# Last six layers: gate and value products of the feed-forward as three fp32r products each, with shared buffers and new orders

## The chip, the cores and the metric

One NeuronCore of a Trainium2 chip runs the whole program. The metric is the device time of one execution in microseconds; lower is better. The engines are TensorE (PE), VectorE (DVE), ScalarE (ACT), GpSimd (POOL) and the sync engine (SP), which only issues DMA transfers here. Each engine works through its own list of instructions in order and is held up by semaphores alone.

## The reference, cut to what matters

The model has four stages on a stream of 4 batches x 512 tokens x 128 features. The change touches the last one, a stack of six layers of windowed attention and gated feed-forward:

```
def ffn_layer(x, g, bln, W1, b1, W2, b2):           # W1: 128 x 682, W2: 341 x 128
    xn = (x - mean) / sqrt(var + 1e-05) * g + bln
    a, gate = split(xn @ W1 + b1, 2)                # two halves of 341 columns
    return a * gelu(gate) @ W2 + b2
for i in range(6):                                   # DEPTH
    x = attn_layer(shift_tokens(x), Wqkv[i], ...) + x    # 16 heads of 64, windows of 32 keys
    x = ffn_layer(shift_tokens(x), ...) + x
```

`shift_tokens` takes half of the features from the token before. All tensors are float32.

## The kernel before

`windowed_layers` (line 1509) holds the six layers. A **round** is one layer for one batch of 512 tokens, so there are 24 rounds; features lie on the partitions. Each engine has a hand-written cyclic order, the table `ORDER`; a word in it is a unit of work, and the dashes behind it say how many rounds late it is: in iteration i of the table, `g0--` works on round i-2. So up to four rounds are under way at once, and the function `turns` walks the table. The units of a round are:

- `P t.j`, `V t.j` (PE, line 1785): queries and keys, and values, of token tile t, four and two products of 128 tokens x 512 columns into the two PSUM banks `psP`. Each is computed as three fp32r products, x_hi·w_hi + x_lo·w_hi + x_hi·w_lo. fp32r is a float32 rounded so that one pass suffices. `w_hi`/`w_lo` and `xh`/`xl` are these splits: a rounded copy by ACT (1858, 1863), and the difference by POOL (2037, 2042).
- `Sq`, `R`, `AB`, `ad`, `Ra`, `nm`: norms and rotary embedding of queries and keys, on ACT, DVE and POOL; `Ve` (ACT) copies the values out. `T t.j` (PE, 1794) transposes the result and `Te` (ACT) copies it out.
- `S k` (PE, 1803 and 1812): scores of 64 queries; `Xm`, `Xe`, `Xd`, `Xn`: maximum (DVE), exponentials (ACT, 1893), sum (DVE), division (POOL, 2071). `At k` (PE, 1823) transposes the probabilities, `Pt` (ACT) copies them out, `Av k` (PE, 1841) multiplies by the values, `Ot` (ACT, 1906) copies out. The transposes of `T` and `At` share one bank `psT`; `Av` has one bank pair `psO`, which `Ot` must have emptied before the next `Av`.
- The tail of a round goes through a single bank `psF`, one after the other: `wo0`, `wo1` (PE, 1729, output projection), `xf` (DVE, residual sum), `xfd` (SP, loads the shifted tokens), `tr` (PE, 1736), `ls`, `lr`, `ln` (layer norm on DVE and POOL), `back` (PE, 1740), `xn` (ACT, 1911), then for each of three column blocks k of 128, 128 and 85 columns `g`k (PE, 1751, gate), `gg`k (ACT, 1917, Gelu, preceded by a load of its table), `a`k (PE, 1751, value), `h`k (DVE, 1994), and at the end `w2` (PE, 1755) and `out` (DVE, 1998).
- SP: `VE k` copies values shifted by 32 tokens into the two buffers `v_even` (lines 1702, 1704; `X` is their name in the profile), `xd` loads the next input of `xh`, `tl` loads `w_o` (1582), `t1` loads the feed-forward weights (1586 to 1588), `wd` loads the next layer's qkv weights.
- The gate and value products at line 1751 are plain float32: one instruction in the code, two records in the profile.

## Time and profile before

| | us |
|---|---|
| three runs | 2397.17, 2399.85 (median), 2401.15 |
| the profiled execution, whole | 2398.7 |
| its span, first to last instruction | 2396.9 |
| PE busy in the span | 2203.9 (92%) |
| ACT busy | 1719.1 (72%) |
| DVE busy | 1780.6 (74%) |
| POOL busy | 1230.9 (51%) |

Busy shares are means over four very different stages. The last stage fills the page's 40 slices from about the 13th on; there the page's PE row shows 9 in nearly every slice and the clock row 9. The ends of matmuls are modelled, so that neighbours overlap in the records; how much room a unit takes on PE is the distance from its start to the next one's.

### The profile page before, as it was taken

To read this page: it belongs to the slowest core of one execution; us is meant where nothing else is said; L and a number is where in the kernel's file an instruction comes from. 1 tells how busy PE (TensorE), PEld (TensorE's weight loads), DVE (VectorE), ACT (ScalarE), POOL (GpSimd) and SP (SyncE) were. 2 spreads that over 40 slices of the span, in tenths; PEclk is the share of its full clock that TensorE was granted. 3 is DMA by queue.
4 is the path that set the end of the run, shared out by engine and by line. 5 is a ranking of instruction groups with operands and counts; after the bars stand their busy time and mean duration, and the time that the engine had idled before them with its cause. 6 is when DMAs were issued, how large, how long until landed. Compare 5 with 4: busy or idle time off the path is not lost.

```text
span 2396.9 us, 82108 instructions
## 1 busy us (share of the span) xinstructions
PE 2203.9 (92%) x33332; PEld 1567.5 (65%) x33332; DVE 1780.6 (74%) x3567; ACT 1719.1 (72%) x3982; POOL 1230.9 (51%) x2002
## 2 busy tenths in 40 slices
PE   6799679999976799999999999999999999999996
PEld 3487368888855566666766666666666666666662
DVE  3577377777777788888888888878888888888851
ACT  2255378888854678878888787777778888778771
POOL 0177010000001677776777776767777777767650
PEclk9899789999987899999999999999999999999997
DMA  2000021221102111112111121112111211122110
GB/s 88 10 1 1 22 98 53 80 80 53 71 2 82 30 51 51 51 47 58 51 53 42 54 72 48 45 44 60 50 41 39 75 53 51 36 64 60 40 33 22
DMA packets 40966, 117.73 MB, mean 49 GB/s; under 512 B 7952, under 2 KB 13392, under 8 KB 37776
## 3 DMA queue, kind: packets, MB, share of 16 engines
q1 hardware_dynamic: 40592, 112.49, 15.5%
q8 instruction: 265, 4.34, 0.8%
q14 instruction: 109, 0.89, 0.1%
HBM read 50.48 MB, written 2.23 MB: 22 GB/s over the span
## 4 chain that ended last, share of the span: by engine, by line
PE 49%; ACT 10%; issue 4%; POOL 2%; DVE 2%; DMA 1%; SPq 0%; ACTq 0%; POOLq 0%; DVEq 0%
PE w_psP L1785 12%; PE w_psT L1794 7%; PE w_psF L1729 6%; PE w_psO L1841 6%; PE w_psS L1812 5%; PE w_psF L1751 5%; PE w_psT L1823 3%; ACT w_pb L1893 3%; PE w_psF L1755 2%; PE w_psS L1803 2%; ACT w_sq L1868 1%; ACT L1893 1%; ACT L1917 1%; DMA w_xsf<-H 1%; ACT w_oT L1906 1%
## 5 line engine op out<-in xcount | busy, mean ns | idle before, releaser
L2055 POOL TENSOR_TENSOR w_ab<-w_ab,w_nrm 128x512 f32<-128x512 f32 x384 | 392.9, 1045 | 8.4 <-POOL w_nrm L84 8.4
L1893 ACT ACTIVATE w_pb<-w_psS,w_mx 128x64 f32<-128x64 f32 x1536 | 350.2, 338 | 2.8 <-DVE w_mx L1962 1.9
L2047 POOL TENSOR_TENSOR w_ab<-w_ab,w_bb 128x512 f32<-128x512 f32 x192 | 245.3, 1278 | 172.8 <-DVE w_bb L1946 171.1
L1958 DVE TENSOR_REDUCE w_nrm<-w_sq 128x8 f32<-128x512 f32 x384 | 249.5, 665 | 107.5 <-ACT w_sq L1868 107.3
L1868 ACT ACTIVATE w_sq<-w_psP 128x512 f32<-128x512 f32 x384 | 237.4, 618 | 84.7 <-DVE w_nrm L1958 42.5
L1785 PE MATMUL w_psP<-w_hi,w_xh 128*128 128x512 f32 x576 | 274.6, 477 | 25.0 <-POOL w_xl L2037 8.5
L2071 POOL TENSOR_TENSOR w_pb<-w_pb,w_sm 128x512 f32<-128x512 f32 x192 | 200.3, 1043 | 185.0 <-DVE w_sm L1971 184.5
L1794 PE MATMUL w_psT<-tables_all,w_ab 128*128 128x128 f32 x1536 | 242.0, 280 | 8.7 <-POOL w_ab L2055 4.0
L1197 DVE TENSOR_TENSOR e_glo<-e_hh,e_ghi 128x512 fp32r<-128x512 f32 x256 | 169.3, 685 | 93.0 <-ACT e_ghi L1151 92.9
L1794 PEld LDWEIGHTS w_psT<-tables_all,w_ab 128*128 128x128 f32 x1536 | 174.2, 141 | 87.3 <-ACT w_qT L1881 23.9
L1785 PE MATMUL w_psP<-w_lo,w_xh 128*128 128x512 f32 x576 | 231.1, 401 | 0.0
L1785 PE MATMUL w_psP<-w_hi,w_xl 128*128 128x512 f32 x576 | 229.3, 398 | 0.0
L1145 ACT ACTIVATE e_hh<-e_psH,e_cols 128x512 f32<-128x512 f32 x256 | 175.4, 686 | 55.4 <-PE e_psH L1067 54.0
L1341 POOL MEMSET a_sc<- 128x256 f32 (+2 forms) x6 | 2.9, 524 | 385.0 <-POOLq L314 385.0
L1899 ACT ACTIVATE w_pT<-w_psT 128x512 f32<-128x512 f32 x192 | 120.5, 628 | 77.0 <-PE w_psT L1823 74.1
L1950 DVE TENSOR_TENSOR w_bb<-w_psP,w_tabs 128x512 f32<-128x512 f32 x192 | 131.6, 685 | 58.6 <-ACT w_sq L1868 49.1
L1812 PE MATMUL w_psS<-w_kT,w_qT 64*32 64x64 f32 x12288 | 168.7, 225 | 5.1 <-issue 4.9
L1729 PE MATMUL w_psF<-w_oT,w_o 128*128 128x512 f32 x384 | 172.5, 592 | 0.9 <-DVE H L1998 0.9
L1751 PE MATMUL w_psF<-w_hh,w 128*128 128x512 f32 (+1 forms) x288 | 155.4, 622 | 7.1 <-ACT w_yn L1917 3.5
L1881 ACT ACTIVATE w_qT<-w_psT 128x512 f32<-128x512 f32 x192 | 115.6, 602 | 64.3 <-PE w_psT L1794 64.2
L1885 ACT ACTIVATE w_kT<-w_psT 128x512 f32<-128x512 f32 x192 | 116.5, 607 | 55.5 <-PE w_psT L1794 55.5
L1812 PEld LDWEIGHTS w_psS<-w_kT,w_qT 64*32 64x32 f32 x12288 | 135.5, 106 | 30.3 <-issue 7.3
(294 smaller groups left out, 5348.5 us busy)
## 6 DMA issues: line engine op xcount, KB each, us to landing
X<-tables_layer SPq DMA_DIRECT2D x48, 384.0 KB, 3.5
X<-w_v SPq DMA_DIRECT2D x48, 384.0 KB, 3.5
e_gb<-gate_rows SPq DMA_DIRECT2D x16, 1024.0 KB, 4.7
e_raw<-in_w_moe SPq DMA_DIRECT2D x32, 256.0 KB, 5.1
w_raw<-in_w_qkv SPq DMA_DIRECT2D x20, 384.0 KB, 4.8
X<-tables_layer SPq DMA_DIRECT2D x48, 128.0 KB, 3.6
w_o<-in_w_o SPq DMA_DIRECT2D x6, 512.0 KB, 4.6
w_xs<-H SPq DMA_DIRECT2D x24, 128.0 KB, 3.3
```

What stands on the lines that cost most here:

```text
L1145: act.activation(hh[b % 2][:, j, :], psH[j][:, :], ACT.Gelu, bias=b1(e, j)).then_inc(s["hh"], 1)
L1729: last = pe.matmul(psF[:, :], w_o[:, pair, :], oT[:, pair, :], start=(pair == 0), stop=(pair == PAIRS - 1), skip_group_check=True)
L1751: last = pe.matmul(psF[0:m, :], w_1[:, at:at + m], xn[:, :], start=True, stop=True)
L1785: last = pe.matmul(psP[u % 2][:, :], x[r % 2][:, tt], w[:, layer % 2, ww], start=(n == 0), stop=(n == len(terms) - 1))
L1794: last = pe.transpose(psT[:, 128 * q:128 * (q + 1)], ab[:, k % 2, j, 128 * q:128 * (q + 1)], c.ident[:, :])
L1812: last = pe.matmul(psS[QB * c4:QB * c4 + QB, h, slot:slot + KEYS], qT[t % 2][rows, 4 * g + c4, at:at + QB], kT[rows, 4 * g + c4, 128 * t + ...
L1868: act.activation(sq[:, i % 2, :], psP[j % 2][:, :], ACT.Square).then_inc(s["sq"], 1)
L1893: last = act.activation(pb[k % 2][:, n, :], psS[:, j, KEYS * q:KEYS * (q + 1)], ACT.Exp, bias=mx[:, n:n + 1])
L1958: dve.tensor_reduce(nrm[k // 2][:, 0, 8 * (i % 8):8 * (i % 8) + 8], sq[:, i % 2, :].rearrange("p (h d) -> p h d", d=DH), AX_X, ALU.add).th ...
L2047: pool.tensor_tensor(a, a, bb[:, i % 2, :], ALU.add).then_inc(s["ad"], 1)
L2055: pool.tensor_tensor(a, a, nrm[k // 2][:, 1, 8 * (i % 8):8 * (i % 8) + 8].unsqueeze(2).to_broadcast([128, 8, DH]), ALU.mult).then_inc(s["n ...
L2071: pool.tensor_tensor(p, p, sm[k % 2][:, :].unsqueeze(2).to_broadcast([128, PAIRS, KEYS]), ALU.mult).then_inc(s["pn"], 1)
```

## The change

The gate and value products `g`k and `a`k become three fp32r products each, like `P` and `V`. For that the layer's `w_1` is split once per layer into `w1_hi` (unit `fh`, ACT) and `w1_lo` (unit `fl`, POOL), and the normalised input of each round into `xn_hi` (unit `xnh`, ACT, a second evaluation from PSUM) and `xn_lo` (unit `xnl`, POOL, the float32 `xn` less `xn_hi`). `g`k now waits for all four. To make room, raw `w_1` is loaded into the space of `hh`, `xn` and the third block of `hh` lie in the space of `yn`, the scratch of the layer norm ahead of the stage lies in `ab`, and two unused tables with their memsets go. All five order tables are new.

```
     xsf = c.sb("w_xsf", [D, N])
-    hh = c.sb("w_hh", [D, 3, N])
-    xn = hh[:, 2, :]
+    hh = c.sb("w_hh", [D, 2, N])
+    xn = gg
+    w_1 = hh[:, :, :].rearrange("p a b -> p (a b)")[:, 0:2 * FF]
+    h_at = (hh[:, 0, :], hh[:, 1, :], gg)
+    xn_hi = c.sb("w_xnh", [D, N], F32R)
+    xn_lo = c.sb("w_xnl", [D, N], F32R)
...
# PE, one line of its table, before and after
-            P1.1 Av2.0- S6.0- At4.0- P1.2 back-- Av3.0- At5.0- P1.3 g0-- S7.0- Av4.0- V1.0 a0-- At6.0-
+            T3.3- S5.0- At3.0- Av2.0- back-- P1.1 S6.0- At4.0- P1.2 Av3.0- At5.0- P1.3 g0-- S7.0- Av4.0-
# SP
-            VE2.0-- xd0.0 VE3.0-- wd0.0- t1-- VE0.0- tl- VE1.0- xfd--""",
+            VE3.0--- xfd--- tl-- xd0.0 VE0.0-- t1--- VE1.0-- VE2.0-- wd0.0-""",
...
                 if f[0] == "g":
-                    pe.wait_ge(s["wf"], (layer + 1) * 48)
-                    pe.wait_ge(s["xn"], r + 1)
+                    pe.wait_ge(s["fh"], layer + 1)
+                    pe.wait_ge(s["fl"], layer + 1)
+                    pe.wait_ge(s["xnh"], r + 1)
+                    pe.wait_ge(s["xnl"], r + 1)
                     wait(pe, s["hh"], 3 * r + k)
...
-                last = pe.matmul(psF[0:m, :], w_1[:, at:at + m], xn[:, :], start=True, stop=True)
+                for n, (w, x) in enumerate(((w1_hi, xn_hi), (w1_hi, xn_lo), (w1_lo, xn_hi))):
+                    last = pe.matmul(psF[0:m, :], w[:, at:at + m], x[:, :], start=(n == 0), stop=(n == 2))
...
+                elif kind == "fh":
+                    if b == 0:
+                        wait(act, s["out"], r)
+                        act.wait_ge(s["wf"], (layer + 1) * 48)
+                        act.activation(w1_hi[:, :], w_1, ACT.Copy).then_inc(s["fh"], 1)
+                elif k == "xnh":
+                    act.wait_ge(s["f"], r * 10 + 3)
+                    wait(act, s["out"], r)
+                    act.activation(xn_hi[:, :], psF[:, :], ACT.Identity, bias=cols[:, 1:2],
+                                   scale=cols[:, 0:1]).then_inc(s["xnh"], 1)
...
+                elif kind == "fl":
+                    if b == 0:
+                        pool.wait_ge(s["fh"], layer + 1)
+                        pool.tensor_tensor(w1_lo[:, :], w_1, w1_hi[:, :], ALU.subtract).then_inc(s["fl"], 1)
+                elif k == "xnl":
+                    pool.wait_ge(s["xn"], r + 1)
+                    pool.wait_ge(s["xnh"], r + 1)
+                    pool.tensor_tensor(xn_lo[:, :], xn[:, :], xn_hi[:, :], ALU.subtract).then_inc(s["xnl"], 1)
```

**PE, from the gate product g0 to the value product a0**, in a round of the second layer. Before (S7 is 1803 with 1812, Av4 and later Av5 are 1841, V is 1785, At6 is 1823):

```order
L1751 MATMUL w_psF<-w_hh,w 128x512
L1803 MATMUL w_psS<-band_bf,ident_bf 128x256 x2
L1812 MATMUL w_psS<-w_kT,w_qT 32x64 x32
L1841 MATMUL w_psO<-w_pT,X 64x32 x32
L1785 MATMUL w_psP<-w_hi,w_xh 128x512
L1785 MATMUL w_psP<-w_hi,w_xl 128x512
L1785 MATMUL w_psP<-w_lo,w_xh 128x512
L1751 MATMUL w_psF<-w_hh,w 128x512
```

After (lines are 10 higher; 1761 is the split product, 1833 is At6, 1851 is Av4 and Av5):

```order
L1761 MATMUL w_psF<-w_xnh,w_1h 128x512
L1761 MATMUL w_psF<-w_xnl,w_1h 128x512
L1761 MATMUL w_psF<-w_xnh,w_1l 128x512
L1813 MATMUL w_psS<-band_bf,ident_bf 128x256 x2
L1822 MATMUL w_psS<-w_kT,w_qT 32x64 x32
L1851 MATMUL w_psO<-w_pT,X 64x32 x32
L1833 MATMUL w_psT<-tables_all,w_pb 128x128 x4
L1795 MATMUL w_psP<-w_hi,w_xh 128x512
L1795 MATMUL w_psP<-w_hi,w_xl 128x512
L1795 MATMUL w_psP<-w_lo,w_xh 128x512
L1851 MATMUL w_psO<-w_pT,w_v 64x32 x32
L1761 MATMUL w_psF<-w_xnh,w_1h 128x512
```

At6 and Av5 have moved in between g0 and a0; the product itself is three instructions.

**ACT, from Ot2 (1906) to the first Gelu load (1917)**, before:

```order
L1906 ACTIVATE w_oT<-w_psO 128x2x8x32
L1858 ACTIVATE w_xh<-w_xs 128x512
L1899 ACTIVATE w_pT<-w_psT 128x512
L1893 ACTIVATE w_pb<-w_psS,w_mx 128x64 x4
L1868 ACTIVATE w_sq<-w_psP 128x512
L1911 ACTIVATE w_hh<-w_psF,w_cols 128x512
L1893 ACTIVATE w_pb<-w_psS,w_mx 128x64 x4
L1899 ACTIVATE w_pT<-w_psT 128x512
L1868 ACTIVATE w_sq<-w_psP 128x512
L1906 ACTIVATE w_oT<-w_psO 128x2x8x32
L1917 ACT_TABLE_LOAD
```

After, from Pt3 (1909) on (1931 is xn, 1926 is xnh, 1916 is Ot2 and Ot3, 1903 the exponentials):

```order
L1909 ACTIVATE w_pT<-w_psT 128x512
L1931 ACTIVATE w_yn<-w_psF,w_cols 128x512
L1878 ACTIVATE w_sq<-w_psP 128x512
L1926 ACTIVATE w_xnh<-w_psF,w_cols 128x512
L1916 ACTIVATE w_oT<-w_psO 128x2x8x32
L1909 ACTIVATE w_pT<-w_psT 128x512
L1903 ACTIVATE w_pb<-w_psS,w_mx 128x64 x8
L1878 ACTIVATE w_sq<-w_psP 128x512
L1916 ACTIVATE w_oT<-w_psO 128x2x8x32
L1878 ACTIVATE w_sq<-w_psP 128x512
L1909 ACTIVATE w_pT<-w_psT 128x512
L1937 ACT_TABLE_LOAD
```

xh has left this stretch (it stands behind the second Gelu now), xnh has come into it, and xn comes one score unit earlier.

**SP, around the load of the shifted tokens w_xsf**, before:

```order
L1708 DMA w_xsf<-H 64x512
L1709 DMA w_xsf<-H 64x511
L1702 DMA X<-w_v 96x1024
L1704 DMA X<-tables_layer 32x1024
L1685 DMA w_xs<-H 64x512
L1686 DMA w_xs<-H 64x511
```

After, in a round where a layer begins (X<-tables_layer 96x1024 is VE0, w_hh is the raw w_1):

```order
L1715 DMA w_xsf<-H 64x512
L1716 DMA w_xsf<-H 64x511
L1692 DMA w_xs<-H 64x512
L1693 DMA w_xs<-H 64x511
L1709 DMA X<-tables_layer 96x1024
L1593 DMA w_hh<-in_w_ff 128x682
L1594 DMA w<-in_w_ff 128x384
```

w_xs and VE0 now stand behind w_xsf, and VE0, which stood a good half round ahead of it, is read by Av0 in the same round.

## Rows read from the trace of the kernel before

**Rows 1.** Page, part 4: share of the chain that ended last, by engine.
```profile
PE 49%; ACT 10%; issue 4%; POOL 2%; DVE 2%; DMA 1%; SPq 0%; ACTq 0%; POOLq 0%; DVEq 0%
```

**Rows 2.** Windows: stretch, us, PE, PEld, DVE, ACT, POOL busy (count), clock, DMA, GB/s.
```profile
1408.66:1434.29 25.63, 24.47 (x595) 18.14 (x594) 20.72 (x40) 24.72 (x63) 18.45 (x37) 1.00 0.19 54
1434.29:1472.56 38.27, 38.18 (x660) 26.06 (x659) 32.36 (x60) 26.96 (x69) 28.45 (x35) 1.00 0.16 44
1399.94:1463.83 63.89, 62.65 (x1252) 44.18 (x1250) 53.07 (x98) 51.68 (x131) 46.90 (x71) 1.00 0.17 48
```

**Rows 3.** Chain in order of time, 1400 to 1480: start, us, what.
```profile
1404.70 0.44 PE w_psF L1736 x4
...
1436.98 0.86 PE w_psF L1751 x2
...
1444.63 1.39 PE w_psP L1785 x6
...
1468.59 0.44 PE w_psF L1736 x4
```

**Rows 4.** Timeline of PE: start, us, instructions, [idle time before <-what ended it].
```profile
1415.90 1.14 PE L1841 MATMUL w_psO<-w_pT,X 64*64 64x32 f32 x64
1417.21 0.28 PE L1803 MATMUL w_psS<-band_bf,ident_bf 32*128 32x256 bf16 x2 [0.18 <-ACT w_pb L1893]
...
1419.93 1.14 PE L1841 MATMUL w_psO<-w_pT,tables_layer 64*64 64x32 f32 x64
1421.00 0.66 PE L1823 MATMUL w_psT<-tables_all,w_pb 128*128 128x128 f32 x4
...
1426.27 0.30 PE L1841 MATMUL w_psO<-w_pT,X 64*64 64x32 f32 x2 [0.94 <-issue]
...
1461.52 0.60 PE L1794 MATMUL w_psT<-tables_all,w_ab 128*128 128x128 f32 x4
```

**Rows 5.** Groups by line: operation, shapes, count | busy us, mean ns | idle.
```profile
L1858 ACT ACTIVATE w_xh<-w_xs 128x512 fp32r<-128x512 f32 x24 | 17.6, 733 | 1.6 <-DMA w_xs<-H 1.6
L1863 ACT ACTIVATE w_hi<-w_raw 128x768 fp32r<-128x768 f32 x20 | 17.1, 855 | 0.0
L2037 POOL TENSOR_TENSOR w_xl<-w_xs,w_xh 128x512 fp32r<-128x512 f32 x24 | 30.6, 1274 | 3.7 <-ACT w_xh L1858 3.7
L2042 POOL TENSOR_TENSOR w_lo<-w_raw,w_hi 128x768 fp32r<-128x768 f32 x20 | 36.8, 1839 | 18.6 <-ACT w_hi L1863 18.5
L1994 DVE SCALAR_TENSOR_TENSOR w_hh<-w_psF,w_cols,w_yn 128x512 f32<-128x512 f32 (+1 forms) x72 | 53.5, 743 | 33.7 <-PE w_psF L1751 33.5
```

**Rows 6.** Timeline of ACT: the table load and the first Gelu of a round.
```profile
1423.84 1.28 ACT L1917 ACT_TABLE_LOAD   x1
1425.13 0.69 ACT L1917 ACTIVATE w_yn<-w_psF,w_cols 128x512 f32<-128x512 f32 x1
```

**Rows 7.** Timeline of POOL: the division Xn5, and the scaling that T2.0 needs.
```profile
1418.68 1.04 POOL L2071 TENSOR_TENSOR w_pb<-w_pb,w_sm 128x512 f32<-128x512 f32 x1
...
1460.06 3.05 POOL L2055 TENSOR_TENSOR w_ab<-w_ab,w_nrm 128x512 f32<-128x512 f32 x3 [0.17 <-POOL w_nrm L84]
```

**Rows 8.** Waits of PE, 900 to 2244: total us, times, longest.
```profile
PE w_psP L1785 <- ACT tables_layer L1875: 5.1, 13, 0.5
...
PE w_psF L1736 <- DMA w_xsf<-H: 3.4, 3, 1.5
```

**Rows 9.** DMA issues by line: count, KB each, median us from issue to landing.
```profile
X<-tables_layer SPq DMA_DIRECT2D x48, 384.0 KB, 3.5
...
w_o<-in_w_o SPq DMA_DIRECT2D x6, 512.0 KB, 4.6
```

**Rows 10.** Line 1702 alone: spread of the time from issue to landing.
```profile
DMA to landing us min/median/max: 3.4/3.5/5.6
```

**Rows 11.** Timeline of PE in the last round, at half the clock.
```profile
2371.07 2.04 PE L1751 MATMUL w_psF<-w_hh,w 128*128 128x512 f32 x2 [0.97 <-issue]
```

**Rows 12.** Timeline of SP: the two loads of the shifted tokens.
```profile
1462.44 0.50 SPq L1708 DMA_DIRECT2D w_xsf<-H  x1
1462.99 0.59 SPq L1709 DMA_DIRECT2D w_xsf<-H  x1
```

65 lines of the change are left out of this document (33 added, 32 removed).

## Prediction, made before the changed kernel ran

> **What bounds the kernel now.** I read the chain of work first, then the last stage by windows, then one round of it unit by unit. The chain belongs to PE for 49% of the whole span, ACT follows with 10% [rows 1]. In the last stage it is tighter. One round takes 63.9 us: the transposes `tr` of two rounds in a row stand in the chain at 1404.70 and 1468.59 [rows 3]. In such a round PE is busy for 62.65 of 63.89 us, DVE 53.07, ACT 51.68, POOL 46.90, at the full clock [rows 2]. So a microsecond taken from PE's work in a round is worth up to a microsecond. But the windows show two phases: from 1434 to 1472 PE is busy for 38.18 of 38.27 us and ACT for 27 of 38, so there PE alone sets the pace; from 1408.66 to 1434.29 ACT is busy for 24.72 of 25.63 us [rows 2]. The tight phase, 1408 to 1434, holds half of the exponentials, the Gelus 0 and 1 with their table loads, and four of the six gate and value products; there PE waits for ACT as soon as ACT gets more to do. A saving of PE outside it is paid out in full, one inside only as far as ACT allows.
>
> **The products.** A float32 product takes 0.86 us of PE in the chain, two P units behind each other 1.39 us, so one triple of fp32r products takes 0.69 us [rows 3]. The triple is the very form that the change uses, in the same shapes, 24 times a round, so its price is not in doubt. Saved: 6 x (0.86 - 0.69) = 1.0 us a round. Behind a transpose the P unit pays some 0.08 us more for its first weights; only a2 gets such a neighbour, so I leave that out. At half the clock, where the last round's six products run (2.04 us of record each [rows 11]), the saving doubles to about 0.34 us each, 2.0 us in all.
>
> Here a rule says more than the row. The Trainium skill, "FP8 and Floating Point Precision", section TensorE Precision Notes, has it that true FP32 takes four passes through the array (high and low halves, all four combinations), and three products of the reduced form then cost three quarters: 0.86 x 0.75 = 0.65 us, an estimate. By it the saving would be 6 x 0.21 = 1.3 us a round instead of 1.0; the row's 0.69 us for three passes decides, and the sum goes by it.
>
> **Neighbours on PE.** Av2 is followed by S6, and S6 starts 1.31 us after it; Av3 is followed by At5, which starts 1.07 us after it [rows 4]. The new order has no S behind an Av: 0.24 us less a round. The rest of PE's units are the same, with about as many transposes behind an S or an Av. Together PE's own work shrinks by 1.0 + 0.24 = 1.24 us a round.
>
> **New work on ACT and POOL.** `xnh` costs what `xh` does, 0.73 us, `xnl` 1.27 us like `xl`, `fh` somewhat less than 0.86 us and `fl` than 1.84 us (682 instead of 768 columns) [rows 5]. ACT goes to 51.7 + 0.7 + 0.8/4 = 52.6 us in a round, POOL to 46.9 + 1.3 + 0.4 = 48.6: both still under PE. What counts is the tight phase. There `xh` (0.73) moves out, to behind the second Gelu, and `xnh` (0.73) moves in, so ACT's load in it stays the same, but for `fh` in one round of four. `g0` waits for xn, xnh, xnl: after `back` that is about 0.8 + 0.7 + 1.3 = 2.8 us, and the order now puts P1.1, S6, At4, P1.2, Av3, At5 and P1.3 between them, over 5 us, where before it was Av3, At5 and P1.3. On POOL `xnl` stands behind Xn5, which ended at 1419.72 (1418.68 + 1.04 [rows 7]), 1.3 us ahead of At5 at 1421.00 [rows 4], and At5 and P1.3 come before g0: `xnl` is hidden. Queued behind it on POOL are ad1.0 and Xn6; POOL is busy for only 18.45 of the 25.63 us [rows 2]. Were g0 late, all of PE would stand behind it, S7 first. Cost of these: nothing. `fh` waits for the load of w_1, which SP issues right behind VE0, some 20 units ahead, and which lands some 3 us later; queued behind `fh` is the copy of V0.1, that frees a bank for P1.1. In the six rounds with `fh` and `fl` ACT has no room for them; half to all of fh's 0.8 us shows, taken 0.5 each: +3 us, between 0 and 5 (with fl's 1.6 us hidden ahead of Xn5, or half of it not).
>
> **New waits.** I walked one round with the units' durations from the timelines, and three places come out late. (a) T2.0 now follows wo1 directly, since V3.0 has moved behind it, so it comes 0.77 us sooner; the scaling on POOL that it needs runs from 1460.06 and is done after a third of its 3.05 us, at 1461.1, and T2.0 started at 1461.52 [rows 4, 7]: slack 0.4, wait 0.4 us. (b) g1 and a1 stood three units apart (Av5, T0.0, P2.1), now two (T0.0, Av6); Gelu 1 waits for its table, 1.28 + 0.69 us [rows 6], behind exponentials and Ot5. My walk gives a wait of 0.8 us before a1, and At7 and P2.1 are queued behind it. Against it, P2.0 no longer waits for the copy of V1.0 (13 times, 0.4 us each [rows 8]), since Av5 now stands between; and stalls like the 0.94 us in which PE had no instruction in Av4 [rows 4] are absorbed by the same slack. (c) g2 needs h1 (0.74 us [rows 5]) and comes 1.8 us after a1 instead of 3.6; T0.2 stands behind `xh` and `wh` on ACT: 0.3 us. Together 1.5 us of new waits, against about 1.1 us of waits in the same stretch before. Taken: +0.4 us a round, between -0.3 (the walk adds up delays that in fact overlap) and +1.2 (none of the old waits goes).
>
> **SP.** VE0, the copy that Av0 reads, stood half a round ahead and now stands behind w_xsf and w_xs. The two loads of w_xsf take 1.1 us to issue and begin when xf is done [rows 12]; w_xs takes as long and some more, and VE0 lands 3.5 us after its issue [rows 9]. By hand: xf is done 1.1 us after the end of wo1, the loads of w_xsf and w_xs are issued by 3.9, VE0 lands at 7.4, and PE arrives at Av0 at 7.8 (thirteen units): hidden by 0.4 us. In the five rounds with a load of w_o (4.6 us, 512 KB [rows 9]) w_xsf no longer stands behind it, which cost `tr` 3.4 us in three rounds [rows 8], but Av0 will wait instead: 0 in sum, between -3 and +8.
>
> **Edges.** First rounds: two memsets less, nothing. Last round: the six products give 2.0 us, `xnh` and `xnl` lie bare, 0.7 + 1.3 = 2.0 us: 0.
>
> **Sum.** Per round -1.0 - 0.24 + 0.4 = -0.84 us; over 23 rounds (the last one stands by itself above) -19.3; +3 for fh and fl. That is -16 us on the profiled execution's 2398.7 (span 2396.9 and 1.8 around it), 1.2 under the median of 2399.85. On the median: 2383.5; forecast **2383**.
>
> **Rivals.**
> 1. *The new waits don't come*: each new one falls into the shadow of another, and all of PE's 1.24 us and a little of the old waits is won, 1.5 us a round: 23 x 1.5 = 35 less 3 gives 2368. For it: PE stands idle for only 1.2 us in a round [rows 2], and most waits are single ones that feed each other. Against: ACT's 96% in the tight phase.
> 2. *ACT sets the pace*: what PE wins in the tight phase turns into waits for Gelu and exponentials, and `xnh` comes on top. Four of the six savings lost, 0.7 us, and 0.5 us more in waits: -1.24 + 0.7 + 0.5, with the fh rounds nothing: 2399. For it: 24.72 of 25.63. Against: load there is equal.
> 3. *VE0 comes late*, slower than before. If the three loads ahead of it slow its landing from 3.5 to the 5.6 us that the longest took [rows 10], Av0 waits 2.1 - 0.4 = 1.7 us in every round: -0.84 + 1.7 = +0.9, over 23 rounds +20, with fh +3: 2423. It decides from a landing of about 4.7 us on (0.84 + 0.4 over 3.5). Against: the four longest are single ones, the median is 3.5 with neighbours on the queue.
> 4. *The split product is no cheaper here*: excluded, the same instructions stand 576 times in the trace.
>
> **How the numbers follow.** Forecast's own range 2374 to 2393, chance 0.60; rival 1 0.22 (2362 to 2374); rival 2 0.10 (2393 to 2405); rival 3 0.08. The range that should hold 8 in 10 leaves out rival 3, most of 2 and the far half of 1: 2366 to 2395. A measurement here can tell 0.2%, 4.8 us, from no change: faster means under 2395.0. Chances: faster 0.83, same 0.09, slower 0.08.
>
> **What would show it.** Right: the triple at 0.69 to 0.77 us from start to start; a round of about 63.0 us between `tr` units; S6 behind At or P at no extra; short waits before a1 and T2.0. Rival 1: rounds near 62.4. Rival 2: ACT busy for over 97% of the stretch from Pt2 to the second Gelu, and more waits of PE for ACT. Rival 3: Av0 waits for the DMA of w_v or tables_layer in most rounds. Wrong altogether: a wait of g0 for POOL, or Gelu table loads beyond four a round.

## The result: 2.2% slower, and where the time went

The changed kernel takes 2451.97 us (median of 4 runs, 2450.23 to 2456.31), the kernel before 2398.51 (2395.68 to 2401.15): ratio 1.0221, 95% interval 1.0201 to 1.0242. Forecast were 2383 us. The profiled execution took 2456.31 us (span 2454.7).

The loss lies in the last six layers. From the first P0.0 of the stage to the P0.0 of round 23 it was 1477.4 us in the trace of before (766.9 to 2244.3) and is 1530.1 now (770.3 to 2300.4): 52.7 us more. This length, called the stage below, serves for all kernels; it is from one profiled execution each.

The page of the changed kernel, part 1 (busy us, share, instructions), part 3 (DMA queues: packets, MB, share) and part 4 (the chain, which answers to [rows 1]):

```profile
PE 2203.2 (90%) x33476; PEld 1611.9 (66%) x33476; DVE 1787.5 (73%) x3567; ACT 1747.1 (71%) x4012; POOL 1273.5 (52%) x2030
...
q8 instruction: 267, 4.37, 0.7%
...
PE 36%; ACT 18%; issue 7%; DVE 5%; DMA 2%; POOL 1%; SPq 1%; ACTq 0%; POOLq 0%; DVEq 0%
```

PE's share of the chain fell from 49% to 36%, and 7% of it is "issue": PE waits for nothing that the profile shows. The waits of PE from 900 to 2240 us (total, times, longest; answers to [rows 8]) say where:

```profile
PE w_psO L1851 <- issue: 38.9, 43, 2.9
PE w_psO L1851 <- DMA X<-tables_layer: 12.3, 5, 2.9
PE w_psF L1736 <- DVE H L2018: 10.4, 20, 0.5
PE w_psF L1761 <- ACT w_yn L1937: 9.3, 20, 0.6
```

The first of these was 8.7 us in 11 waits before:

```profile
PE w_psO L1841 <- issue: 8.7, 11, 1.9
```

Line 1851 is the product of the weights with the values (`Av`), 64 small products in a unit. The timeline of PE (start, us, instructions, idle time before) and three stretches of it by windows (columns as in [rows 2]):

```profile
1439.33 0.32 PE L1851 MATMUL w_psO<-w_pT,tables_layer 64*64 64x32 f32 x2 [2.28 <-issue]
...
1502.95 0.40 PE L1795 MATMUL w_psP<-w_lo,w_xh 128*128 128x512 f32 x1
1503.28 0.28 PE L1813 MATMUL w_psS<-band_bf,ident_bf 32*128 32x256 bf16 x2
1503.49 0.29 PE L1822 MATMUL w_psS<-w_kT,w_qT 64*32 64x64 f32 x3
1504.07 0.83 PE L1822 MATMUL w_psS<-w_kT,w_qT 64*32 64x64 f32 x61 [0.28 <-issue]
1504.83 0.66 PE L1833 MATMUL w_psT<-tables_all,w_pb 128*128 128x128 f32 x4
1505.41 1.13 PE L1851 MATMUL w_psO<-w_pT,tables_layer 64*64 64x32 f32 x62
1509.12 0.24 PE L1851 MATMUL w_psO<-w_pT,tables_layer 64*64 64x32 f32 x2 [2.58 <-issue]
...
1576.32 0.24 PE L1851 MATMUL w_psO<-w_pT,tables_layer 64*64 64x32 f32 x2 [1.75 <-issue]
```
```profile
1439.33:1509.12 69.79, 65.08 (x1256) 47.46 (x1256) 54.54 (x101) 53.26 (x132) 50.75 (x74) 0.96 0.17 46
...
1438.80:1445.60 6.80, 6.27 (x21) 5.08 (x21) 3.14 (x8) 2.98 (x8) 2.82 (x3) 0.50 0.03 10
1510.50:1513.90 3.40, 3.39 (x11) 2.72 (x11) 0.44 (x1) 2.53 (x8) 0.08 (x1) 0.50 0.00 0
```

PE does 62 of the 64 products of Av1, stands for 1.5 to 2.9 us with two left, and goes on. No semaphore stands inside a unit, so this is no wait for data. It happens in 17 of the 24 rounds, always at this product. After 14 of these 17 stops the granted clock is 0.5, the lower level, for some microseconds (here for 6.8 us from 1438.8 and for 3.4 us from 1510.5), and what PE does there takes up to twice as long. From 900 to 2240 us PE spends 51 us at that level, against 7 us before. In the first round of each layer the stop is missing; there Av0 waits 2.0 to 2.9 us for the copy VE0 instead. And wo0 waits half a microsecond in nearly every round for `out`, behind Xd0.0 on DVE.

The mechanism stands in the numbers of the page. The queue "instruction" moved 4.37 MB in 267 packets, 16.4 KB each. PE's queue holds 33476 products, as many weight loads and some 1450 instructions that only wait: 68,400 in all, so 64 bytes each and 256 to a packet. Between two stops there are 1256 products and 1256 weight loads (the window from 1439.33 to 1509.12 above) and 48 waiting instructions: **2560, ten times 256**. Before, a round had 1250 of each and 45: 2545. The six triples bring 12 instructions more, the new waits 3. So the ends of the packets, which moved on by 15 instructions each round before, now stand at the same places in every round, and one of them is the 62nd product of Av1. The 256 instructions up to there (most of S4, At2, and Av1 to its 62nd product) are only 2.5 us of work.

In all 17 stops of this kind PE went on 1.3 to 1.6 us after the last 16 KB packet had landed (at 1507.76 for 1509.12). That the 256 are so short is not enough for a stop: in the first rounds of the layers the same 256 took 2.2 to 3.0 us, and PE ran on. There the packet had started 0.2 to 2.0 us before PE came to the 256 (PE had just waited for VE0), in the 17 stops it started 1.4 to 2.9 us after. So "held up by semaphores alone", as the section on the chip has it, leaves out the supply of instructions.

The Trainium skill, "Runtime: NRT & Kernel Launch", section Instruction fetch mechanics, says that the sequencer fetches blocks of 16 KiB, 256 instructions; the trace agrees. It also says that the cost of crossing such a boundary is "mostly hidden"; here it is not, with 1.5 to 2.9 us at a time.

Not all of the 38.9 us is this. Counted over all units of PE, idle times that end just behind a packet's end (at instruction 192 to 195 of a 256, 1.2 to 1.6 us after a packet had landed) are 34.1 us from 900 to 2240 us, for 14.2 us before, where units other than Av were hit as well. Another 5.6 us stand at the first product of Av3, 0.2 to 0.4 us in nearly every round, where no packet ends: Av3 starts there 0.1 us after the copy Ot2 on ACT, which the new `xnh` pushes back. The profile calls both "issue".

### The profile page after: what moved, and what is told of

It reads as the page before. It is cut to its first block, busy times and chain, and to the rows that moved or that the text cites. A ratio compares the mean times of both kernels' runs of the same rounds, so it can differ in the third digit from the quotient of the medians.

```text
span 2454.7 us, 82554 instructions
## 1 busy us (share of the span) xinstructions
PE 2203.2 (90%) x33476; PEld 1611.9 (66%) x33476; DVE 1787.5 (73%) x3567; ACT 1747.1 (71%) x4012; POOL 1273.5 (52%) x2030
## 3 DMA queue, kind: packets, MB, share of 16 engines
q8 instruction: 267, 4.37, 0.7%
## 4 chain that ended last, share of the span: by engine, by line
PE 36%; ACT 18%; issue 7%; DVE 5%; DMA 2%; POOL 1%; SPq 1%; ACTq 0%; POOLq 0%; DVEq 0%
PE w_psP L1795 10%; PE w_psF L1736 7%; PE w_psT L1804 6%; ACT w_pb L1903 5%; PE w_psS L1822 4%; PE w_psO L1851 3%; PE w_psF L1761 3%; ACT w_sq L1878 3%; ACT L1903 2%; PE w_psT L1833 2%; ACT L1937 2%; ACT w_pT L1909 2%; ACT w_yn L1937 1%; DMA X<-tables_layer 1%; PE w_psS L1813 1%
## 5 line engine op out<-in xcount | busy, mean ns | idle before, releaser
L1978 DVE TENSOR_REDUCE w_nrm<-w_sq 128x8 f32<-128x512 f32 x384 | 256.1, 674 | 61.0 <-ACT w_sq L1878 61.0
L1878 ACT ACTIVATE w_sq<-w_psP 128x512 f32<-128x512 f32 x384 | 246.2, 641 | 53.3 <-PE w_psP L1795 25.4
L1804 PE MATMUL w_psT<-tables_all,w_ab 128*128 128x128 f32 x1536 | 250.0, 287 | 9.1 <-ACT w_qT L1891 4.0
L1804 PEld LDWEIGHTS w_psT<-tables_all,w_ab 128*128 128x128 f32 x1536 | 184.1, 145 | 86.6 <-ACT w_qT L1891 28.0
L1795 PE MATMUL w_psP<-w_lo,w_xh 128*128 128x512 f32 x576 | 236.3, 410 | 0.0
L1795 PE MATMUL w_psP<-w_hi,w_xl 128*128 128x512 f32 x576 | 234.9, 408 | 0.0
L1982 DVE TENSOR_REDUCE w_mx<-w_psS 128x8 f32<-128x512 f32 x192 | 130.5, 680 | 81.6 <-PE w_psS L1822 81.4
L1989 DVE TENSOR_REDUCE w_sm<-w_pb 128x8 f32<-128x512 f32 x192 | 130.7, 681 | 43.8 <-ACT w_pb L1903 41.7
L1155 ACT ACTIVATE e_ghi<-e_hh 128x512 fp32r<-128x512 f32 x256 | 153.9, 630 | 0.0
```

The source lines that it names most:

```text
L1795: last = pe.matmul(psP[u % 2][:, :], x[r % 2][:, tt], w[:, layer % 2, ww], start=(n == 0), stop=(n == len(terms) - 1))
L1804: last = pe.transpose(psT[:, 128 * q:128 * (q + 1)], ab[:, k % 2, j, 128 * q:128 * (q + 1)], c.ident[:, :])
L1878: act.activation(sq[:, i % 2, :], psP[j % 2][:, :], ACT.Square).then_inc(s["sq"], 1)
L1978: dve.tensor_reduce(nrm[k // 2][:, 0, 8 * (i % 8):8 * (i % 8) + 8], sq[:, i % 2, :].rearrange("p (h d) -> p h d", d=DH), AX_X, ALU.add).th ...
```

## Experiments

Medians, and the stage as defined above. Each group ran on one chip with the kernel before beside it; its median went from 2396 to 2402. The stage comes from the profiled execution, and its whole time is not always near the median: above it for the changed kernel (2456.3), e3 (2459.1), e9 (2461.8) and e11 (2415.8), below it for e5 (2431.2), e10 (2422.5) and e17 (2404.1).

| run | us | ratio, 95% interval | stage, us |
|---|---|---|---|
| before | 2398.5 | 1 | 1477.4 |
| changed kernel | 2452.0 | 1.022 (1.020, 1.024) | 1530.1 |
| e1 products alone, old orders | 2409.3 | 1.006 (1.004, 1.007) | 1483.7 |
| e2 changed, old SP | 2460.7 | 1.025 (1.020, 1.030) | 1532.5 |
| e3 changed, `out` first | 2445.2 | 1.021 (1.018, 1.024) | 1526.9 |
| e4 before, new SP | 2496.1 | 1.042 (1.040, 1.044) | 1572.7 |
| e5 new orders alone | 2441.4 | 1.018 (1.014, 1.022) | 1510.5 |
| e6 changed, Av1 later | 2445.7 | 1.018 (1.012, 1.023) | 1518.9 |
| e7 e1, g0 after S7 | 2403.8 | 1.003 (1.002, 1.005) | 1480.5 |
| e8 before, dense stretch | 2442.9 | 1.019 (1.015, 1.022) | 1520.2 |
| e9 changed, stream shifted | 2457.0 | 1.023 (1.020, 1.027) | 1519.2 |
| e10 before, ends at Av4 | 2428.4 | 1.011 (1.007, 1.015) | 1487.6 |
| e11 before, ends elsewhere | 2411.5 | 1.005 (1.003, 1.007) | 1466.6 |
| e12 e1, back earlier | 2406.1 | 1.002 (1.000, 1.004) | 1481.9 |
| e13 as e11, no pause | 2394.3 | 0.999 (0.997, 1.000) | 1470.3 |
| e14 e12, xh and xl moved | 2415.9 | 1.008 (1.006, 1.011) | 1490.4 |
| e15 changed, VE0 and `out` early | 2426.4 | 1.012 (1.009, 1.016) | 1504.9 |
| e16 e12, xh behind gg0 | 2402.9 | 1.001 (0.999, 1.004) | 1481.4 |
| e17 e16, Ve1.0 first | 2409.2 | 1.004 (1.002, 1.006) | 1486.6 |
| e18 xnh on DVE | 2397.7 | 0.999 (0.998, 1.001) | 1474.8 |

### Orders or products, SP or PE (e1 to e5)

**e1_products_alone.**
```diff
+ act:  ... Ot1.0-- fh0.0--- Ve0.1- ...  xn--- xnh--- Xe6.1-- ...
+ pool: ... Xn4.0-- fl0.0--- ad1.0- Xn5.0-- xnl--- ad1.2- ...
```


> The changed kernel's code with the order tables of the kernel before; only the four new words are put in (fh0.0--- behind Ot1.0--, xnh--- behind xn---, fl0.0--- behind Xn4.0--, xnl--- behind Xn5.0--). Theory (the loss sits in the orders, the products are a gain): six products a round at 0.69 for 0.86 us are 1.0 us, 24 rounds 24 us, less some 3 us for fh and fl: 2378 us, between 2370 and 2386. Rival (the added ACT and POOL instructions or the waits g0 has on them eat the gain, so that the new orders were needed to hide them): 2395 to 2410, and the waits of PE in front of g0 name ACT or POOL.

Measured 2409.3: the rival. The timeline of PE at g0, and further on at g2, and the waits of PE from 900 to 2240 us:

```profile
1553.07 0.47 PE L1762 MATMUL w_psF<-w_xnh,w_1h 128*128 128x512 f32 x1 [1.49 <-POOL w_xnl L2071]
...
1566.70 0.39 PE L1762 MATMUL w_psF<-w_xnh,w_1h 128*85 128x512 f32 x1
1566.93 0.39 PE L1762 MATMUL w_psF<-w_xnl,w_1h 128*85 128x512 f32 x1
1567.16 0.39 PE L1762 MATMUL w_psF<-w_xnh,w_1l 128*85 128x512 f32 x1
1567.40 0.38 PE L1805 MATMUL w_psT<-tables_all,w_ab 128*128 128x128 f32 x2
```
```profile
PE w_psF L1762 <- POOL w_xnl L2071: 31.3, 21, 1.6
```

The triple costs 0.70 us from start to start (1566.70 to 1567.40), as forecast. (With its new instructions a round of e1 is 2560 too, but its packets' ends stand where they cost next to nothing, 1.2 us from 900 to 2240.) But 1.5 us of wait a round for `xnl` stand against 1.0 us of saving. In the old order three units stand between `back` and g0; the chain xn, xnh, xnl needs more. This the new orders do hide: the changed kernel has no such wait but in the last round.

**e2_old_sp_queue.**
```diff
- VE3.0--- xfd--- tl-- xd0.0 VE0.0-- t1--- VE1.0-- VE2.0-- wd0.0-
+ VE2.0-- xd0.0 VE3.0-- wd0.0- t1-- VE0.0- tl- VE1.0- xfd--
```


> The changed kernel with SP's table alone put back to that of before (VE2, xd, VE3, wd, t1, VE0, tl, VE1, xfd). Theory A (the new SP order releases w_xsf, w_xs, VE0, VE1, VE2 and w_raw together, some 2 MB in 10 us, and behind them both VE0 and the instructions of TensorE land late): the waits of PE for issue in front of the w_psO products fall from 41 us to under 12, those of Av0 for VE0 from 12 us to nothing, and the half-clock stretches behind them go too: 2451 less 60 to 75, so 2377 to 2392 us. Theory B (the new PE order puts Av0, S4, At2 and Av1 so close that their instructions cannot be supplied at that rate, whatever SP does): the waits for issue stay near 41 us, only Av0's waits for VE0 go with their share of half clock: 2430 to 2438 us.

Measured 2460.7 (2441.8 to 2465.5). The two waits of PE that count, 900 to 2240 us:

```profile
PE w_psO L1851 <- issue: 42.1, 45, 2.5
...
PE w_psF L1743 <- DMA w_xsf<-H: 10.2, 5, 2.4
```

Theory A, the burst of transfers, is dead: the waits for issue stay at 42 us with the old queue. Theory B was right on that, but not on the time: `tr` now waits for w_xsf behind the load of w_o nearly as long (10.2 us) as Av0 had waited for VE0 (12.3).

**e3_out_first.**
```diff
- ... AB3.1- Xd0.0- out--- R3.1- ...
+ ... AB3.1- out--- Xd0.0- R3.1- ...
```


> The changed kernel with one word moved: on DVE out stands ahead of Xd0.0 again. Theory (wo0 waits 0.5 us more in 21 rounds since its DVE operation out is queued behind Xd0.0): the wait of PE for H in front of w_psF falls from 10.9 us to under 2 and the time from 2451 by 10 to 15 us, to 2436 to 2442. Rival (the stalls further on are timed by the transfers and not by PE, so what is won at wo0 is waited for behind Av1): 2448 to 2453.

Measured 2445.2 (2439.5 to 2459.1), between the two. The wait for `out` is gone from the waits of PE, and the stage is shorter by 3 us where 10.4 were waited. From start to start wo0 and S2.0 now stand 3.72 us apart in the median, wo1 and T2.0 3.65, for 3.53 and 3.43 in the kernel before and 3.60 and 3.44 in the changed one; why these eight products run slower there I did not find.

**e4_new_sp_in_before.**
```diff
- VE2.0-- xd0.0 VE3.0-- wd0.0- t1-- VE0.0- tl- VE1.0- xfd--
+ VE3.0--- xfd--- tl-- xd0.0 VE0.0-- t1--- VE1.0-- VE2.0-- wd0.0-
```


> The kernel before with SP's table alone taken from the changed kernel (VE3, xfd, tl, xd, VE0, t1, VE1, VE2, wd); its products and its other orders stay. Theory A (the burst of transfers starves TensorE of instructions): the waits of PE for issue in front of the w_psO products rise from 9 us to 30 or more, Av0 waits for VE0 as well, and the time rises from 2399 to between 2430 and 2460 us. Theory B (it is the new order on PE): the waits for issue stay under 12 us; the time is 2397 to 2410.

Measured 2496.1, worse than either theory. Waits of PE, 900 to 2240 us:

```profile
PE w_psO L1841 <- DMA X<-tables_layer: 64.2, 19, 6.6
...
PE w_psO L1841 <- issue: 4.0, 7, 1.4
```

So the new SP queue does delay VE0, by 3.4 us a round in an order where Av0 comes before `tr`, but it starves PE of nothing: 4.0 us of issue.

**e5_new_orders_alone** (the tables of the changed kernel in the kernel before, without fh, fl, xnh, xnl).

> The kernel before (its plain products) with all five order tables of the changed kernel, without the four new words. Theory (the orders carry the whole loss, and more than the difference, since the products give some back): the waits for issue in front of the w_psO products stand near 45 us, and the time is the changed kernel's 2452 plus the 1.0 us of products in 24 rounds less some 3 us of conversion, 2465 to 2478 us. Rival (the split products with their ACT and POOL steps cost time in the new orders, not only in the old): under 2455 us.

Measured 2441.4: less than the changed kernel, not more. Waits of PE, 900 to 2240 us:

```profile
PE w_psO L1841 <- DMA X<-tables_layer: 21.8, 11, 3.7
PE w_psO L1841 <- issue: 12.5, 18, 1.8
PE w_psF L1729 <- DVE H L1998: 10.6, 20, 0.5
```

The same orders without the 15 instructions a round wait 12.5 us for issue instead of 38.9 (over all units, at packets' ends, 17.8 for 34.1). They also wait only 0.8 us before a1, for 9.3, and nothing before Av3, for 5.6: so with the split products 14 us, 0.7 us a round, come back as waits in the changed kernel itself: PE reaches a1 sooner, and ACT, with `xnh` in its list, later. PE stops in rounds 17 and 18 near the end of Av1, when the moving end of the 256s gets there (after 54 and 62 of its 64 products), and once more when it has moved on, one product into V0.0. That was the lead to the packets. My reading in the expectation, that the products would give back 20 us, failed since they also fix the packets' ends at the worst place.

### The place of the packets' ends (e6, e8 to e11, e13)

**e6_av1_later.**
```diff
- ... S4.0- At2.0- Av1.0- T3.1- V0.0 T3.2- ...
+ ... S4.0- At2.0- V0.0 T3.1- Av1.0- T3.2- ...
```


> The changed kernel with one unit of PE moved: V0.0 and T3.1 stand ahead of Av1.0 again as in the kernel before (S4, At2, V0.0, T3.1, Av1), instead of behind it (S4, At2, Av1, T3.1, V0.0). Putting SP's old queue back left the stall of 2 to 3 us behind Av1 as it was, so the theory is now that Av0, S4 and Av1, 64 small products each, stand within 3.8 us and PE's instructions do not come as fast. Theory: with 1.3 us more ahead of Av1 the wait behind it falls from 2.3 us to under 1 in most rounds and the half-clock stretches go with it: 2452 less 35 to 60, so 2392 to 2417 us. Rival (a place in the program or another cause makes PE wait there once a round, and the wait moves to the next dense place, S5 or Av2): 2440 to 2455 us.

Measured 2445.7: the rival. The stops moved and split (timeline of PE, one round):

```profile
1429.65 0.36 PE L1851 MATMUL w_psO<-w_pT,tables_layer 64*64 64x32 f32 x9 [0.72 <-issue]
...
1435.65 0.67 PE L1851 MATMUL w_psO<-w_pT,X 64*64 64x32 f32 x32 [0.80 <-issue]
...
1442.14 1.30 PE L1851 MATMUL w_psO<-w_pT,tables_layer 64*64 64x32 f32 x49 [1.90 <-issue]
```

Av1 after 55 products, Av2 after 32, Av3 after 15 of 64: in the records they are 256 instructions apart, and the places are the same in each round, though not each of the three stops comes in each.

**e8_dense_in_before.**
```diff
- ... At1.0- Av0.0- T2.3- tr-- P0.2 T3.0- P0.3 S4.0- At2.0- V0.0 T3.1- Av1.0- T3.2- ...
+ ... At1.0- T2.3- tr-- P0.2 Av0.0- T3.0- P0.3 S4.0- At2.0- Av1.0- V0.0 T3.1- T3.2- ...
```


> The kernel before with its products, its SP queue and all other orders, and on PE only the stretch from Av0 to T3.1 written as the changed kernel has it: T2.3, tr, P0.2, Av0, T3.0, P0.3, S4, At2, Av1, then V0.0 and T3.1. Theory (density of the small products): PE waits for issue behind Av1 by 1.5 to 3 us in most rounds, the half clock follows it, and the time rises by 35 to 60 us to 2435 to 2460 us. Rival (the stall needs something else of the new orders): under 2410 us.

Measured 2442.9, in the range of the theory and for another reason. No stop in Av1 (5 waits of `w_psO` for issue in all, 5.1 us). My order put transposes behind one another, T2.3 behind At1 and T3.2 behind T3.1, and each waits for the copy that frees the one bank `psT`:

```profile
1421.41 0.66 PE L1794 MATMUL w_psT<-tables_all,w_ab 128*128 128x128 f32 x4 [0.75 <-ACT w_pT L1899]
...
1430.29 0.66 PE L1794 MATMUL w_psT<-tables_all,w_ab 128*128 128x128 f32 x4 [0.75 <-ACT w_qT L1881]
```

Two times 0.75 us in 24 rounds are 36 of the 46 us. As a test of the theory the run is spoilt, but it holds one fact against the simplest form of it: in round 18 an end did stand at the end of Av1, and PE did not stop. The packet had been fetched from 2027.98 on, 0.7 us ahead of PE's start on the 256 instructions before it; in the stops of the changed kernel it is fetched 1.4 to 2.9 us after PE has begun them. What makes the sequencer ask early or late I do not know.

**e9_shifted_stream** (448 waits on a semaphore that has arrived, ahead of the first round).

> The changed kernel with 224 more instructions in PE's queue, once, ahead of the first round (448 waits on a semaphore that has long arrived, two to an instruction); orders, products and rounds as they are. In the trace of the changed kernel a round is 2560 PE instructions, ten times 256, the instructions are fetched in packets of 16 KB (256 of 64 bytes), and PE stops each round at the same place, 62 products into Av1, at the same position 192 of 256. Theory (each stop is a packet of instructions that comes late, and which place it hits is set by where the 256s begin): with the stream shifted by 224 the boundary falls 32 instructions later, behind V0.0, and others fall elsewhere in the round; the stop of 2.3 us inside Av1 is gone, smaller ones of under 1 us may come at Av2, and the time is 2452 less 25 to 45 us, 2407 to 2427 us. Rival (Av1 is too dense wherever the packets begin): Av1 keeps its wait, 2445 to 2460 us.

Measured 2457.0, in the rival's range and not in the theory's; the stage is 1519.2, 10.9 shorter, but it begins 18 us later (788.2 for 770.3): the added waits are not free. The stop in Av1 is gone, as the theory said. But others came, one for nearly each dense place in reach (timeline of PE, one round):

```profile
1448.37 0.69 PE L1822 MATMUL w_psS<-w_kT,w_qT 64*32 64x64 f32 x45 [1.24 <-issue]
...
1457.82 0.43 PE L1851 MATMUL w_psO<-w_pT,X 64*64 64x32 f32 x16 [0.66 <-issue]
...
1464.10 0.71 PE L1851 MATMUL w_psO<-w_pT,tables_layer 64*64 64x32 f32 x33 [1.69 <-issue]
```

I had the mechanism and the wrong size: waits at packets' ends are 30.2 us over all units, for 34.1. Of the 38.9 us of waits for issue in front of `w_psO` 24.7 stay, and 5.5 are new in front of `w_psS`; most of it only moves. From Av0 to Av1 stand 414 instructions in 7.3 us, so some end of 256 falls among them wherever the count begins.

**e10_before_locked_dense** and **e11_before_locked_sparse**, the decisive pair: the kernel before, its round filled up to 2560 instructions, with the ends at two different places.
```diff
+ behind wo0, each round:       for _ in range(30): pe.wait_ge(s["z"], 2)
+ ahead of the first round:     for _ in range(242): ...     (e10; two waits to an instruction)
+ ahead of the first round:     for _ in range(484): ...     (e11)
```


> The kernel before with 15 more PE instructions in each round (30 waits behind the first four wo products) so that its round, too, is 2560 instructions, and 121 once ahead of the first round, so that the end of a 256 stands 62 products into Av4 in every round. In its own trace the ends of the 256s move by 15 a round and PE stopped at one of them in about 12 rounds, for 0.7 to 2.1 us, among them at this place (0.9 us at 1426.27). Theory: PE now stops there by 0.9 to 1.3 us in nearly every round: 12 to 25 us over e11_before_locked_sparse, 2410 to 2430 us. Rival (the position in the stream means nothing): within 4 us of e11_before_locked_sparse.

> As e10_before_locked_dense, with 242 in place of 121 instructions once ahead of the first round: the same rounds, the same number of instructions in each, only the ends of the 256s stand 121 instructions earlier in every round, where the kernel before ran without a stop in its rounds 17 and 18. Theory: hardly a stop for issue over 0.6 us in any round, 2385 to 2402 us (the 15 instructions a round cost 0 to 0.5 us each round). Rival: as e10.

Measured 2428.4 and 2411.5. The waits of PE from 900 to 2240 us in e10, and one of the stops:

```profile
PE w_psO L1843 <- issue: 27.2, 24, 1.6
PE w_psS L1814 <- issue: 10.7, 22, 0.9
```
```profile
1380.60 1.13 PE L1843 MATMUL w_psO<-w_pT,X 64*64 64x32 f32 x62
1382.82 0.30 PE L1843 MATMUL w_psO<-w_pT,X 64*64 64x32 f32 x2 [1.08 <-issue]
```

And of e11:

```profile
PE w_psO L1843 <- issue: 1.1, 2, 0.9
```

Same kernel, same instructions in each round; only 121 more or less of them ahead. With the end at the 62nd product of Av4, PE stops there in every round, 0.7 to 1.6 us; with the ends 121 instructions earlier there are 1.1 us of such waits in all. The stages differ by 21 us, the medians by 17 in spite of a pause at the start of e11 that is 14 us longer (the two profiled executions by 7 only, which is 21 less 14). PE's waits at packets' ends are 37.8 us in e10 and 1.1 us in e11. This shows the cause: where the packets end decides whether PE stops. The level of e11 was missed by 9 us: its 242 instructions ahead cost 27 us (first product at 793.9).

**e13_before_unpadded_phase** (e11 with the waits left out in round 0 and none ahead).

> The rounds of e11_before_locked_sparse without its cost at the start: the kernel before, 15 more PE instructions in each round but the first, none ahead of the first round, so that the ends of the 256s stand in every round within one instruction of where they stood in e11. In e11 the first product of the stage came at 793.9 us for 766.9 in the kernel before (27 us of waits), and from there to the last round it took 1466.6 us for 1477.4. Theory (the kernel before, too, loses some 11 us to instruction packets, and the place of their ends is all that matters): 2411 less 27, 2380 to 2390 us, under the kernel before by 0.4 to 0.8%. Rival (e11's rounds were shorter for another reason, such as the pause at the start): 2396 to 2403 us.

Measured 2394.3, ratio 0.9985 (0.997 to 1.0001): 2 us under the kernel before, where I wanted 10 or more: between the two forecasts. The stage is 7 us shorter than before, as 8.7 us of waits for issue allow, and of it some 4 are given back at its start and end. The kernel before loses at most 7 us to its packets; its round has a floor of 63.8 us, which e11 and e13 reach and before nearly did.

### How the 53 us divide (e15)

**e15_ve0_and_out_early.**
```diff
- sp:  VE3.0--- xfd--- tl-- xd0.0 VE0.0-- ...
+ sp:  VE3.0--- VE0.0-- xfd--- tl-- xd0.0 ...
- dve: ... AB3.1- Xd0.0- out--- R3.1- ...
+ dve: ... AB3.1- out--- Xd0.0- R3.1- ...
```


> The changed kernel with two places repaired and the rest as it is: on SP VE0 stands ahead of xfd (it no longer waits for xf), and on DVE out stands ahead of Xd0.0. Theory: Av0's waits for VE0 at the first round of each layer go (12 us and some 5 us of half clock behind them), wo0's too (11 to 14 us), and the stops for issue inside Av1 stay, since nothing here moves the ends of the 256s: 2452 less 15 to 30, 2422 to 2437 us. Rival (the two have the same root as Av1's stop, or PE waits at Av1 for what it wins before it): 2442 to 2455 us.

Measured 2426.4, inside the forecast. Of the waits of PE from 900 to 2240 us two are left that count:

```profile
PE w_psO L1851 <- issue: 45.0, 52, 2.6
PE w_psF L1761 <- ACT w_yn L1937: 9.2, 19, 0.6
```

So VE0 and `out`, with the half clock behind Av0, are 25 us. Of the 30 us that stay against before the stops for issue are the greater part: at packets' ends PE waits 40.1 us, for 14.2 before, 26 more, and it spends 31 us at half clock, for 7. The rest is a1's wait of 9.2 us and Av3's of 6.3, and the split products give nothing back that shows. The run also tests the link between the late packet and Av0: now that Av0 does not wait, PE stops inside Av1 in the first rounds of the layers too, for 2.0 to 2.6 us, so in all of rounds 1 to 22.

### Are the split products a gain (e7, e12, e14, e16 to e18)

All from e1, with the helpers given other places.

**e7_g0_after_s7** (PE: `P1.3 S7.0- g0--` for `P1.3 g0-- S7.0-`).

> The run of the products alone (e1_products_alone) with g0 and S7.0 exchanged on PE. There PE waited 1.6 us in each round in front of g0 for w_xnl on POOL, which ends 0.2 us before g0 starts. Theory: S7 (1.0 us) fills that wait, g0 starts when it did, a0 comes 1.0 us closer behind g0 and still finds gg0 done: 1.0 to 1.1 us in 24 rounds, 2409 less 25, so 2380 to 2387 us, and under the kernel before. Rival (a0 now waits for gg0 on ACT, or S7's Av4 meets the instruction supply): 2395 to 2410 us.

Measured 2403.8, the rival. S7 itself waits now, for the exponentials Xe6 that stand behind xn and xnh on ACT, 0.8 us a round (16.6 of the 20.5 us; the rest is S6), and P2.0 for the copy of V1.0:

```profile
PE w_psS L1814 <- ACT w_pb L1904: 20.5, 42, 0.8
PE w_psP L1796 <- ACT tables_layer L1886: 9.4, 26, 0.6
```

**e12_back_earlier.**
```diff
- pe:  ... Av2.0- S6.0- At4.0- P1.2 back-- Av3.0- ...
+ pe:  ... Av2.0- back-- S6.0- At4.0- P1.2 Av3.0- ...
- act: ... Pt3.0-- Ot2.0-- xh0.0 Pt4.0-- Xe6.0-- Sq1.2- xn--- xnh--- Xe6.1-- ... Pt6.0-- Ot4.0-- ...
+ act: ... Pt3.0-- xn--- Ot2.0-- xnh--- Pt4.0-- Xe6.0-- Sq1.2- Xe6.1-- ... Pt6.0-- xh0.0 Ot4.0-- ...
```


> The run of the products alone (e1_products_alone, 2409 us) with the chain in front of g0 started earlier: on PE back stands right behind Av2, 2.4 us earlier, where ln on DVE has long ended (1543.89 for back at 1548.59 in that run); on ACT xn stands behind Pt3, xnh behind Ot2, and xh0.0 is moved from ahead of Pt4 to behind Pt6. Theory (the products' gain was lost in g0's wait of 1.5 us a round for w_xnl, and nowhere else): the wait goes, 24 times 1.0 to 1.5 us, 2409 less 24 to 36 us: 2373 to 2385 us, under the kernel before by 0.5 to 1%. Rival (ACT is full in this stretch, so what xn and xnh take earlier Xe6 and Pt4 give back, and S7 or At5 waits in g0's place): 2395 to 2410 us.

Measured 2406.1, the rival. The wait for `xnl` is gone; Av5 waits 0.7 us a round for Ot4 (14.0 us, which the profile calls issue), and V1.1 comes 0.6 us later, 0.35 us of it idle.

**e14_products_no_wait** (e12 with xh0.0 ahead of wh0.0, xl0.0 behind wl0.0, Sq1.2 ahead of Xe6.0).

> e12_back_earlier with its two new waits taken out: there Av5 waited 0.76 us a round for an operation of ACT behind the moved xh0.0, and V1.1 0.6 us for the square Sq1.2 that xn and xnh push back. Here xh0.0 goes to wh0.0 and xl0.0 behind wl0.0, and Sq1.2 stands ahead of Xe6.0 again. Theory (the split products are worth 1.0 us a round once no engine's order makes PE wait for their helpers): 2406 less 15 to 30 us, 2376 to 2391 us. Rival (ACT is full between Av2 and g0, and each placement of its 1.4 us more leaves PE a wait of 0.5 us or more a round somewhere): 2396 to 2410 us, with the waits of PE at another name.

Measured 2415.9, worse than either. T1.0 (0.5 us a round), T0.3 (0.2) and P2.0 (0.5) wait instead:

```profile
PE w_psP L1796 <- ACT tables_layer L1886: 9.5, 23, 0.6
PE w_psT L1805 <- POOL w_ab L2082: 9.1, 18, 0.5
```

**e16_xh_behind_gg0** (e12 with Sq1.2 ahead of Xe6.0 and xh0.0 behind gg0).

> e12_back_earlier with Sq1.2 ahead of Xe6.0 (as in the kernel before) and xh0.0 behind gg0; xl0.0 stays where it was. In e12 PE waited 0.76 us a round at Av5 for Ot4 behind xh0.0, and 0.6 us at V1.1; in e14 the waits came back at T1.0 (0.66 us), T0.3 (0.4 us) and Av4, behind POOL's later xl0.0. Theory (the products are worth 1.0 us a round where ACT's and POOL's helpers find a place): both waits of e12 go and none of e14's comes: 2406 less 20 to 32, 2374 to 2386 us. Rival (ACT is full from Ve0.1 to Xe7, with a table load of 1.28 us in it, and 1.4 us more a round shows up at PE wherever it is put): 2396 to 2412 us.

Measured 2402.9, the rival; the wait has moved to P2.0:

```profile
PE w_psP L1796 <- ACT tables_layer L1886: 20.6, 26, 1.0
```

**e17_ve1_first** (e16 with Ve1.0 ahead of Xe7.0).

> e16_xh_behind_gg0 with Ve1.0 ahead of Xe7.0 on ACT. In e16 P2.0 waited 1.1 us a round for Ve1.0, which stood behind Xe7.0, and a table load of 1.28 us ahead of that. Theory A (ACT is full from Ve0.1 to gg1; an order only chooses which product of PE waits for it): P2.0's wait goes, a1 waits as much longer for gg1, 2396 to 2406 us, as e16. Theory B (only the place was wrong, the split products are worth 1.0 us a round): 2403 less 15 to 25, 2378 to 2388 us.

Measured 2409.2, 3 us above theory A. P2.0's wait is gone (18.0 us in e16), and PE waits in front of Av5 instead (30.3 us, for 3.4). The profile puts it down to issue, but this is no packet: Ot4 on ACT, which Av5 needs, ends at 1432.50 (timelines of ACT and PE):

```profile
1431.84 0.66 ACT L1917 ACTIVATE w_oT<-w_psO 128x512 f32<-128x512 f32 x1
```
```profile
1432.60 0.61 PE L1852 MATMUL w_psO<-w_pT,w_v 64*64 64x32 f32 x28 [1.41 <-issue]
```

Theory A holds but for that: ACT is full between Ve0.1 and gg1, with its table loads of 1.28 us, and each order only chooses the product that waits (I had named a1; it was Av5). In the rows of e12, e14 and e16 ACT is busy for 99.5% of this stretch of 19 us, in the kernel before for 97.5%. One such stretch of e16 by windows (columns as in [rows 2]):

```profile
1413.84:1432.95 19.11, 17.55 (x440) 12.84 (x438) 13.72 (x25) 19.02 (x48) 15.50 (x23) 1.00 0.25 72
```

**e18_xnh_on_dve.**
```diff
- act: ... xn--- xnh--- ...
+ dve: ... Xm6.0- xnh-- AB1.1 ...      dve.tensor_scalar(xn_hi[:, :], xn[:, :], 1.0, 0.0, ALU.mult, ALU.add)
  pe:  back-- behind Av2.0-;  act: xn--- behind Pt3.0--
```


> The split products with the orders of the kernel before, but xnh is a DVE operation on xn (behind Xm6.0) in place of an ACT operation on psF, so that ACT has nothing more in a round than in the kernel before (but fh, once a layer); on PE back stands behind Av2 and on ACT xn behind Pt3, so that xn, xnh and xnl end before g0. Theory A (it was ACT's 0.7 to 1.4 us a round that took the gain): most of the 1.0 us a round comes through, 2397 less 10 to 22 us, 2375 to 2387 us. Theory B (the split products do not pay in this kernel, whatever engine makes their halves; DVE's 0.7 us then delays the norms and PE waits for those): 2395 to 2410 us.

Measured 2397.7, ratio 0.9992 (0.9978 to 1.0006): the best place for the products, and no gain that can be measured. P1.3 now waits for DVE, 0.6 us a round, which is about what the moved step adds there:

```profile
PE w_psP L1796 <- DVE w_ab L1969: 12.2, 21, 0.7
```

That is theory B. Taking the step from ACT gave 7 us of the stage against e12 (and ACT's share of its full stretch is back at 97.4%), so ACT was a part of the loss, but then the saving on PE ends at the next engine. Packets do not hide a gain here: PE waits 1.6 us at their ends in e18 and 2.5 in e13, the kernel before with as many instructions a round, and the stage of e18 is 4.5 us longer than that of e13. None of the kernels beats the one before by more than the measurement can tell.

## Why the prediction was wrong, point by point

**What bounds the kernel.** Read right for PE's windows, and read too kindly. "PE 62.65 of 63.89" says that PE is nearly full, not that a microsecond less on PE makes the round shorter. e11 and e18 show rounds of 63.8 and 64.1 us whether PE has the plain or the cheaper products. ACT's 24.72 of 25.63 us in the tight phase [rows 2] was the number to build on.

**The products.** The term 1.0 us a round was right as PE time (0.70 us measured for the 0.69 of the sum, [rows 3]), and wrong as time of the kernel: with the helpers, in every order tried, the kernel came out between 19 us over the kernel before (e14) and 2 us under it (e18, less than can be told from nothing), never 24 under it. The step that failed is "Cost of these: nothing" together with full payment of the saving: in the changed kernel 0.7 us of the 1.0 us a round came back as waits before a1 and Av3, which the same orders without the split and its helpers do not have (e5). Rival 2, ACT sets the pace, 2399 us, is near what e16 and e18 measured for the products in the old orders (2402.9, 2397.7), and I had given it 0.10; in e18, though, it is DVE that PE waits for.

**Neighbours.** S6 now starts 0.9 us behind P1.1 and pays nothing for it, as forecast; the 0.24 us went the way of the products' saving.

**g0.** Right for the changed kernel: g0 does not wait for POOL, and e1 shows what it would cost without the moved `back` (1.5 us).

**New waits.** (b) came, smaller, 0.3 to 0.6 us before a1, 9.3 us in 20 waits, and for another reason than the order, since e5 has 0.8 us of it. (a) and (c) did not come, T2.0, g2 and T0.2 do not wait. The old wait of P2.0 went, as forecast. One was missed altogether: on DVE Xd0.0 had moved ahead of `out`, and wo0 waits 0.5 us for it in nearly every round, 10.4 us; I had walked ACT, POOL and PE and of DVE only its busy time.

**SP.** The right place, half the size. VE0 lands in 3.8 us in the median where the sum had 3.5, and in 5.4 to 6.2 us in the five rounds with a load of w_o ahead of it (the page's row puts VE0 and VE1 together, and VE1 took 4.5). In rounds without that load Av0 hides it, as forecast, if only by 0.1 to 0.2 us, and in the five with one it does not (12.3 us where the sum had 0, range up to +8). Rival 3 wanted this in every round.

```profile
X<-tables_layer SPq DMA_DIRECT2D x48, 384.0 KB, 4.5
...
w_o<-in_w_o SPq DMA_DIRECT2D x6, 512.0 KB, 5.1
```

**What stood nowhere in the sum.** PE's supply of instructions: 34.1 us of waits at packets' ends for 14.2, 20 more, and half the clock behind 14 of the 17 stops in Av1. The row was on my table, the 0.94 us in Av4 with two products left [rows 4], and I called it a stall that slack would absorb. That is the second step that failed. Had I asked why PE stops inside a unit, the counts x1252 and x1250 of one round [rows 2] and the size of the packets on the page would have led to 256, and the new counts to 2560.

**In sum**: from -16 to +53 are 69 us. The experiments give: products not paid, about 18 (the sum had -23 and +3 for them, e18 measured -2); VE0 and `out`, with their half clock, 25 (e15); packets that end in Av1, about 26 (e15 waits 40.1 us at packets' ends for 14.2 before). That this adds up to 69 is partly luck: the three overlap, since a wait removed in one place shows partly at the next, the half clock behind the packets' stops is not priced by itself, and the medians of the runs are good to a few us each. No run takes the phase alone out of the changed kernel: e9 shifts it and moves the stops, and the decisive pair is built on the kernel before.

## What to carry to other kernels

When most of a kernel's instructions are small, count PE's instructions: 256 make a packet, a loop whose round is a multiple of 256 meets the packets' ends at the same places for ever, and where 256 of them run in 2.5 us PE stopped in 17 rounds of 22 here, and did not where the packet had been fetched ahead. A wait for "issue" in the middle of a unit is this; one at the start of a unit with several semaphores may be an engine. And a saving on the busiest engine is worth what the second one lets through: price it with the helper steps in the second engine's fullest stretch, not in its average.

## What the runs showed of the hardware

- PE's instructions come in packets of 16 KB, 256 instructions. After a late one PE went on 1.3 to 1.6 us after it had landed, in 17 stops of 17. The same place in the program, inside Av4, cost 0.05 or 1.1 us a round, depending only on how many instructions stood ahead of it (e11, e10).
- Instructions on PE that wait for a semaphore which has long arrived are not free: 121 of them ahead of the stage cost 13 us (e10), 224 cost 18 (e9), 242 cost 27 (e11); the 15 a round of e11, behind wo0, cost nothing that can be seen (rounds of 63.8 us).
- An idle time of PE of 1.5 to 2.9 us was in most cases (14 of the 17 stops in Av1) followed by a stretch at a granted clock of 0.5, the lower level (rows from 1438.8 and 1510.5 above); with stops of about 1.1 us, as in e10, the clock fell once from 900 to 2240 us.
- Open: when the sequencer asks for the next packet. In e8, and in the first rounds of the changed kernel's layers, the packet was on its way before PE began the 256 instructions, in the 17 stops 1.4 to 2.9 us after.
